# Expert layer: three of the four pieces of the down product as three float32r products each

## The reference, cut to what matters

```
def _moe(x, gate_w, w1, w2, w3):
    ...
    rw, sel = jax.lax.top_k(logits, TOP_K)
    rw = jax.nn.softmax(rw.astype(jnp.float32), axis=-1).astype(x.dtype)
    ...
    for e in range(E):
        we = jnp.sum(jnp.where(sel == e, rw, 0.0), axis=-1)
        h = jax.nn.silu(xf @ w1[e].T) * (xf @ w3[e].T)
        out = out + h @ w2[e].T * we[:, None]
```

## Time and profile before

| | |
|---|---|
| median of 3 runs | 3040.33 us (3038.86 to 3045.66) |
| the profiled execution: its own time | 3042.93 us |
| the profiled execution: span from first to last instruction | 3041.2 us |
| TensorE, share of the span busy | 94% |
| VectorE, ScalarE, GpSimd | 75%, 61%, 23% |
| start of `experts` in the span | 2311.7 us |

### The profile page before, as it was taken

The page is one execution under the profiler, slowest core; times in us unless marked ns, Lnnn a source line. Parts: engine busy times, 40 slices in busy tenths (PEclk is TensorE's granted clock), DMA queues, the critical chain, the costliest instruction groups (busy, mean ns, idle before and its releaser), DMA issues. The chain is left out here.

```text
span 3041.2 us, 62526 instructions
## 1 busy us (share of the span) xinstructions
PE 2866.5 (94%) x22877; PEld 1805.0 (59%) x22878; DVE 2282.8 (75%) x4028; ACT 1867.4 (61%) x3491; POOL 689.7 (23%) x964
## 2 busy tenths in 40 slices
PE   5999999986999999999999999998978999999997
PEld 4777777774333333333333333336767888888886
DVE  5777776774999999999999999976876555555553
ACT  3666666662888888888888888885533222222221
POOL 2222222222000000000000000001102555555554
PEclk7899998986999999999999999998889999999999
DMA  1223322224222222222222222216742333333332
GB/s 46 84 98 112 110 99 98 103 79 131 60 74 72 87 67 67 66 73 72 67 63 71 72 70 67 64 44 189 238 137 73 51 52 50 50 52 50 50 52 37
DMA packets 170749, 243.11 MB, mean 80 GB/s; under 512 B 30920, under 2 KB 118240, under 8 KB 170512
## 3 DMA queue, kind: packets, MB, share of 16 engines
q1 hardware_dynamic: 121920, 170.57, 18.0%
q0 software_dynamic: 31152, 52.33, 8.7%
q10 hardware_dynamic: 17440, 16.98, 1.7%
HBM read 126.53 MB, written 111.21 MB: 78 GB/s over the span
## 5 line engine op out<-in xcount | busy, mean ns | idle before, releaser
L1030 DVE TENSOR_REDUCE b_mxq<-b_p_m 128x1 f32<-128x1024 f32 x1024 | 1220.8, 1221 | 76.3 <-PE b_p_m L1057 67.1
L964 ACT ACTIVATE b_probs<-b_p_e 128x512 f32<-128x512 f32 x2048 | 1105.8, 597 | 140.4 <-PE b_p_e L1110 36.6
L1057 PE MATMUL b_p_m<-b_kst,b_qst 64*128 64x512 f32 x1536 | 568.2, 449 | 0.8 <-DVE b_mxq L1030 0.8
L1110 PE MATMUL b_p_e<-b_qst,b_kst 64*128 64x512 f32 x1536 | 559.9, 444 | 0.2 <-ACT b_probs L964 0.2
L1082 PE MATMUL b_p_o<-b_probs,b_vst 128*32 128x256 f32 x6160 | 481.9, 390 | 0.5 <-ACT b_probs L964 0.4
L1110 PEld LDWEIGHTS b_p_e<-b_qst,b_kst 64*128 64x128 f32 x1536 | 236.4, 184 | 312.5 <-ACT b_probs L964 266.1
L1851 ACT COPY d_hT<-d_p_h 128x512 f32<-128x512 f32 x136 | 79.8, 587 | 401.4 <-PE d_p_h L1944 386.6
L1082 PEld LDWEIGHTS b_p_o<-b_probs,b_vst 128*32 128x32 f32 x6160 | 126.3, 108 | 243.6 <-issue 133.1
L1821 POOL DMA_INDIRECT out_dram<-d_y,d_to x136 | 217.7, 1601 | 199.5 <-DVE d_y L1895 97.4
L1952 PE MATMUL d_p_y<-w2T,d_hT 128*128 x1088 | 257.1, 379 | 1.5 <-ACT d_hT L1851 1.5
L1057 PEld LDWEIGHTS b_p_m<-b_kst,b_qst 64*128 64x128 f32 x1536 | 234.0, 185 | 15.8 <-DVE b_mxq L1030 12.4
(11 more groups left out here) (317 smaller groups left out, 4582.4 us busy)
## 6 DMA issues: line engine op xcount, KB each, us to landing
b_qst<-qk_d SPq DMA_DIRECT2D x288, 64.0 KB
b_kst<-qk_d SPq DMA_DIRECT2D x288, 64.0 KB
qk_d<-a_hi SPq DMA_DIRECT2D x32, 512.0 KB, 2.8
qk_d<-a_lo SPq DMA_DIRECT2D x32, 512.0 KB, 3.8
v_d<-a_v_s SPq DMA_DIRECT2D x16, 1024.0 KB, 4.6
o_d<-b_oT POOLq DMA_DIRECT2D x63, 256.0 KB, 2.7
b_vst<-v_d SPq DMA_DIRECT2D x48, 256.0 KB
raw<-in_L_ffn_w_dram SPq DMA_DIRECT2D x24, 512.0 KB, 5.1
```

The costliest lines, as they stand in the source:

```text
L964: nc.scalar.activation(probs[(2 * step + e % 4 // 2) % BUFS][:, (e % 2) * 512:(e % 2 + 1) * 512], p_e[(slot(e) if more1 else e) % EB][:], ...
L1030: V_.reduce_max(mxq[half][:, h, qt:qt + 1], p_m[j % 2][:], AX.X).then_inc(s["m_red"], 1)
L1057: mm(p_m[j % 2][:, kh * 512:(kh + 1) * 512], qst[r][rows(h), qt * P:(qt + 1) * P], kst[r][rows(h), kh * 512:(kh + 1) * 512], start=True, s ...
L1110: mm(p_e[u % EB][:], kst[r][rows(h), kt * P:(kt + 1) * P], qst[r][rows(h), a * 512:(a + 1) * 512], start=True, stop=True).then_inc(s["e_ps ...
```

## The change

1. `SPLIT = 3`. For the pieces k = 0, 1, 2 the down product is made of three float32r products: rounded hT by rounded w2, rounded hT by the rest of w2, rest of hT by rounded w2. The piece k = 3 stays one float32 product.
2. The rounded parts and rests of w2 (`w2_hi`, `w2_lo`) are made at the beginning of `experts`: ScalarE rounds 768 columns of each expert into a scratch (`rounded`) and copies them back into `w2_hi`, VectorE subtracts. `w2_hi` is declared in the place that `w2T` was declared in, so the fourth piece is still read as `w2T`.
3. ScalarE's copy of the transposed `h` becomes two: 128 columns plain, 384 columns rounded. VectorE gets a new step for each tile, `transposed_low`, that subtracts the rounded part from what is in PSUM. `down` waits for it (`hT_lo`).
4. `act_s`, `h` and `hT` have one buffer instead of two. The small tiles lie in the `raw` buffers of earlier stages. So the Silu waits for the product before it (`h_done`), and `product(m)` for `inner_transposes(m-1)` (`hT_ps`).
5. VectorE's order for a tile is evacuate(m-2), product(m), transposed_low(m-1), scaled(m+2), shared(m+2).

```
+    SPLIT = 3
+    w2_hi = sb("w2_hi", [P, NE, I // P, D], f32r)
+    w2_lo = sb("w2_lo", [P, NE, SPLIT, D], f32r)
-    act_s, h = [sb(f"act{r}", [P, I]) for r in range(2)], [sb(f"h{r}", [P, I]) for r in range(2)]
-    hT = [sb(f"hT{r}", [P, 4, P]) for r in range(2)]
+    hT = sb("hT", [P, 2, SPLIT, P], f32r)
+    hT_hi, hT_lo = hT[:, 0], hT[:, 1]
+    act_s, h = raw[1][:, 0:I], raw[1][:, I:2 * I]
+    rounded = [raw[1][:, 0:SPLIT * D].bitcast(f32r), hT[:].rearrange("p a k t -> p (a k t)")]
...
     def _(act):
+        def weights(e):
+            if e > 1:
+                act.wait_ge(s["w2_rest"], e - 1)
+            nc.scalar.copy(rounded[e % 2], w2T[:, e, 0:SPLIT].rearrange("p k n -> p (k n)")).then_inc(s["w2_round"], 1)
+        def weights_back(e):
+            act.wait_ge(s["w2_rest"], e + 1)
+            nc.scalar.copy(w2_hi[:, e, 0:SPLIT].rearrange("p k n -> p (k n)"), rounded[e % 2].bitcast(f32)).then_inc(s["w2_done"], 1)
+        for e in range(NE):
+            if e > 1:
+                weights_back(e - 2)
+                act.wait_ge(s["w2_done"], e - 1)
+            weights(e)
+        weights_back(NE - 2)
+        weights_back(NE - 1)
+        act.wait_ge(s["w2_done"], NE)
...
         def activated(m, r):
             act.wait_ge(s["up_ps"], 2 * m + 1)
-            nc.scalar.activation(act_s[r][:], p_up[r][:, 0], ACT.Silu).then_inc(s["act_done"], 1)
+            act.wait_ge(s["h_done"], m)
+            nc.scalar.activation(act_s, p_up[r][:, 0], ACT.Silu).then_inc(s["act_done"], 1)
         def transposed(m, r):
             act.wait_ge(s["hT_ps"], m + 1)
-            nc.scalar.copy(hT[r][:], p_h[:]).then_inc(s["hT_done"], 1)
+            nc.scalar.copy(hT_whole, p_h[:, SPLIT:4])
+            nc.scalar.copy(hT_hi, p_h[:, 0:SPLIT]).then_inc(s["hT_done"], 1)
...
     def _(dve):
+        for e in range(NE):
+            dve.wait_ge(s["w2_round"], e + 1)
+            V_.tensor_tensor(w2_lo[:, e].rearrange("p k n -> p (k n)"), w2T[:, e, 0:SPLIT].rearrange("p k n -> p (k n)"), rounded[e % 2].bitcast(f32), ALU.subtract).then_inc(s["w2_rest"], 1)
...
         def product(m, r):
             dve.wait_ge(s["act_done"], m + 1)
             dve.wait_ge(s["up_ps"], 2 * m + 2)
-            V_.tensor_tensor(h[r][:], act_s[r][:], p_up[r][:, 1], ALU.mult).then_inc(s["h_done"], 1)
+            dve.wait_ge(s["hT_ps"], m)
+            V_.tensor_tensor(h, act_s, p_up[r][:, 1], ALU.mult).then_inc(s["h_done"], 1)
+        def transposed_low(m):
+            dve.wait_ge(s["hT_done"], m + 1)
+            V_.tensor_tensor(hT_lo, p_h[:, 0:SPLIT], hT_hi.bitcast(f32), ALU.subtract).then_inc(s["hT_lo"], 1)
...
-                product(m, q % 2)
                 if not first or q > 1:
                     evacuate(m - 2, (q + 2) % 4)
+                product(m, q % 2)
+                if not first or q > 0:
+                    transposed_low(m - 1)
...
         def down(m, r, e):
             pe.wait_ge(s["hT_done"], m + 1)
+            pe.wait_ge(s["hT_lo"], m + 1)
             pe.wait_ge(s["y_done"], m)
-            for k in range(4):
-                last = mm(p_y[:, 0:D], hT[r][:, k], w2T[:, bass.ds(e, 1), k, :].rearrange("p o n -> p (o n)"), start=(k == 0), stop=(k == 3))
+            for k in range(SPLIT):
+                for j, (a, w) in enumerate(((hT_hi, w2_hi), (hT_hi, w2_lo[:]), (hT_lo, w2_hi))):
+                    mm(p_y[:, 0:D], a[:, k], w[:, bass.ds(e, 1), k, :].rearrange("p o n -> p (o n)"), start=(k == 0 and j == 0), stop=False)
+            for k in range(SPLIT, 4):
+                last = mm(p_y[:, 0:D], hT_whole[:, k - SPLIT], w2T[:, bass.ds(e, 1), k, :].rearrange("p o n -> p (o n)"), start=False, stop=(k == 3))
             last.then_inc(s["y_ps"], 1)
```

More of the change, by code:

```diff
@@ L1760, in _, with experts @@
                 column(e * per + i)
-def experts(nc, ctx, ident, xg_d, up_hi, up_lo, w2T, ln2_w, token_of, pick, expert_of, out_d, TILES):
+def experts(nc, ctx, ident, xg_d, up_hi, up_lo, w2T, raw, ln2_w, token_of, pick, expert_of, out_d, TILES):
     P, D, I, NE = 128, 256, 512, 8
@@ L1774, in sb @@
         return ctx.enter_context(nc.sbuf_tensor("d_" + name, shape, dt))
[L1776 to L1779, removed]
+    SPLIT = 3
+    w2_hi = sb("w2_hi", [P, NE, I // P, D], f32r)
+    w2_lo = sb("w2_lo", [P, NE, SPLIT, D], f32r)
     xh, xl = [sb(f"xh{r}", [P, 2, P], f32r) for r in range(2)], [sb(f"xl{r}", [P, 2, P], f32r) for r in range(2)]
-    act_s, h = [sb(f"act{r}", [P, I]) for r in range(2)], [sb(f"h{r}", [P, I]) for r in range(2)]
-    hT = [sb(f"hT{r}", [P, 4, P]) for r in range(2)]
-    y = [sb(f"y{r}", [P, D]) for r in range(2)]
+    hT = sb("hT", [P, 2, SPLIT, P], f32r)
+    hT_hi, hT_lo = hT[:, 0], hT[:, 1]
+    act_s, h = raw[1][:, 0:I], raw[1][:, I:2 * I]
+    y = [raw[2][:, r * D:(r + 1) * D] for r in range(2)]
+    hT_whole = raw[2][:, 2 * D:2 * D + (4 - SPLIT) * P].rearrange("p (k t) -> p k t", k=4 - SPLIT)
+    xs = [raw[2][:, 640:640 + D + 2], *(raw[0][:, r * (D + 2):(r + 1) * (D + 2)] for r in range(3))]
+    small = raw[0][:, 3 * (D + 2):]
+    ln2, ids = small[:, 0:2], small[:, 2:8].bitcast(i32)
+    tok, to = [ids[:, r:r + 1] for r in range(4)], [ids[:, 4 + r:5 + r] for r in range(2)]
+    part, share = [small[:, 8 + 2 * r:10 + 2 * r] for r in range(4)], [small[:, 16 + r:17 + r] for r in range(4)]
+    rounded = [raw[1][:, 0:SPLIT * D].bitcast(f32r), hT[:].rearrange("p a k t -> p (a k t)")]
     p_x = ctx.enter_context(nc.psum_tensor("d_p_x", [P, 4, P], f32))
@@ L1913, in _ @@
         round(TILES // 4 - 1, False, 2)
-        for m in (TILES - 2, TILES - 1):
-            evacuate(m, m % 4)
+        evacuate(TILES - 2, 2)
+        transposed_low(TILES - 1)
+        evacuate(TILES - 1, 3)
     @block.tensor
@@ L1943, in inner_transposes @@
             for k in range(4):
-                last = tr(p_h[:, k, :], h[r][:, k * P:(k + 1) * P], ident[:])
+                last = tr(p_h[:, k, :], h[:, k * P:(k + 1) * P], ident[:])
             last.then_inc(s["hT_ps"], 1)
@@ L1966, in round @@
                 up(m, r, e)
+                if first and q == 2:
+                    pe.wait_ge(s["w2_done"], NE)
                 if not first or q > 1:
@@ L2012, in layer_kernel @@
                                 ln1_w, wq, wk, wv, x1_d, norm, qk_d, v_d, pair0, B)
-        raw = [sb(f"raw{j}", [P, 1024]) for j in range(3)]
+        raw = [sb(f"raw{j}", [P, 1024])[:] for j in range(3)]
         slots = sb("slots", [P, 2 * NT])
@@ L2025, in layer_kernel @@
             up_hi, up_lo = (weights.enter_context(nc.sbuf_tensor(n, [P, NE, 2, D // P, I], mybir.dt.float32r)) for n in ("up_hi", "up_lo"))
-            w2T = weights.enter_context(nc.sbuf_tensor("w2T", [P, NE, I // P, D], f32))
+            down = ExitStack()
+            w2T = down.enter_context(nc.sbuf_tensor("w2T", [P, NE, I // P, D], f32))
             with Stage(nc) as stage:
                 invert_places_and_transpose_weights(nc, stage, ident, ones_r, lower_r, slots, counts, raw, token_of, pick, expert_of, w1, w3, w2, up_hi, up_lo, w2T, NT, TILES)
+            down.close()
             with Stage(nc) as stage:
-                experts(nc, stage, ident, xg_d, up_hi, up_lo, w2T, ln2_w, token_of, pick, expert_of, out_d, TILES)
+                experts(nc, stage, ident, xg_d, up_hi, up_lo, w2T, raw, ln2_w, token_of, pick, expert_of, out_d, TILES)
 _INS = ["L0_attn_x", "L0_attn_Wq", "L0_attn_Wk", "L0_attn_Wv", "L0_attn_Wg", "L0_attn_Wgk1", "L0_attn_Wgk2",
```

28 lines of the change are left out of this document (14 added, 14 removed).

## The result

The changed kernel took 3023.43 us in the median of 4 runs (3017.12 to 3027.36), the kernel before 3041.56 (3038.86 to 3045.66). The ratio is 0.9937, with a 95% interval from 0.9915 to 0.9959: faster by 0.63%, where 0.7% and 3020 us had been forecast. The profiled execution took 3027.36 us, its span is 3025.6.

The account below looks back on a forecast made before the run. TensorE was taken to bound the last stage, 5.19 us per tile. From the profiled 3042.93 us, minus 29.1 (down products) plus 8.0 (beginning) gave 3021.8; the median, 2.6 lower, 3019.2, stated as 3020, range 3011 to 3033.

Parts of the forecast that it names:

- The down product: TensorE, each tile of the last stage: 1.50 us in place of 1.72, saving 29.1 us over 134 tiles.
- the rival of short products that the sequencer can't issue fast enough: TensorE's down product: nine more instructions cost 1.2 us per tile, making the kernel slower at 3210 us; chance 0.06.
- The shorter price: Down product by the skill's 109 ns per 256-column product: another 0.09 us saved per tile, sum some 12 us lower.
- The waits and the new VectorE step: Single-buffer waits and transposed_low in each tile: cost nothing, covered by up, with 1.55 us least slack; subtraction 0.55 us.
- The beginning: Start of `experts`: ScalarE's sixteen copies and VectorE's subtractions delay scaled(0) and the whole stage by 8.0 us.
- The table load: ScalarE, beginning of `experts`: 1.28 us, ending with the last copies back at about 2326.4, ahead of the first Silu.
- The pauses at lap tops: TensorE's sequencer late from three expert-number loads: 1.36 us in each of 16 laps, 22 us, kernel at 3042; chance 0.08.
- my case: Whole kernel: tile of 4.97 us with TensorE busy 100 of 100, beginning 8.0 us later, 3020 us; chance 0.78.
- A load's price: TensorE's register loads at lap tops: by the skill's 600 ns, three take 1.8 us, showing 0.2 per lap, 3 in all.
- The ring of scatters: GpSimd's scatters become the bound if landings beside gathers exceed 4.10 us: 3048 at 4.32, 3073 at 4.5; chance 0.05.
- My argument that slow landings would show in the period: Against scatters becoming the bound: landings beside gathers today can't exceed 4.3 us, or the tile period would show it.

Follow-up runs that it names:

- Waits only: The kernel before with only single `act_s`, `h` and `hT`, their two new waits and VectorE's new order: 3042.57 us, ratio 1.0005.
- loads late: The changed kernel with two of TensorE's three expert-number loads at a lap's top moved behind the first up product: 3011.75 us, 0.9900 of the kernel before.
- early inputs: The changed kernel with VectorE splitting the first two inputs behind the third and fifth subtraction of weights: 3021.06 us, 0.9934 of the kernel before.
- both: The changed kernel with later expert-number loads at lap tops and earlier splits of the first two inputs: 3008.56 us, 0.9899 of the kernel before.

## Why the prediction was right

- **The down product**, forecast at 1.50 us from the 256-column products of the first stage (0.119 each): measured 1.51. The whole forecast hangs on this term, 29 us, and it held. So the rival of short products that the sequencer can't issue fast enough is out: they start 0.12 us apart, though their addresses come from registers.
- **The shorter price** of 109 ns for 256 columns, which the Trainium skill gives ("TensorE: Matmul & The Clock Gate", Back-to-back issue gap), would have made it 1.41 us by an estimate of 0.43 + 9 x 0.109. The trace shows 119, and the measurement decides.
- **The waits and the new VectorE step** at nothing: right. Forecast 1.55 us of slack, measured 1.53; the subtraction 0.55, measured 0.56. Waits only shows the buffers' part by itself, in the kernel before.
- **The beginning**, forecast 8.0 us: measured 7.9. ScalarE's copies take 0.83 us and 1.60 from one expert to the next (1.61 forecast). The table load was misplaced: I took it to end at 2326.4, but it stands behind the wait for up(0) and runs only then. It delayed the first product of VectorE by a quarter us against the kernel before and TensorE not at all.
- **The pauses at lap tops** were a rival with a chance of 0.08 and a price of 22 us. They came, with 9.9 us. This is the step that failed: I held my case and this rival to exclude each other, and my case has TensorE busy 100 of 100 us, where 98.5 were measured. Its mechanism, a fixed number and not a time, is what the traces show. Its price was wrong in the reserve: I counted a dozen products, 1.61 us, and the queue held 17 records, 2.19 us. Against it stood 2.97 us for three loads, and the sequencer needed 2.93. That agreement is luck: a load costs 0.65 and not 0.99, and the rest is the jump and register work, which I had left out.
- **A load's price.** That a load takes 0.65 us agrees with the Trainium skill ("DMA: Bandwidth & Descriptors", Latency and other measured facts), which has about 600 ns at least. By it I had 3 us over the stage, from loads of 1.8 us against a reserve of 1.61; both sides of that comparison were too small.
- **Up** got 0.055 us shorter per tile, some 7.4 us over the stage, not forecast by any case. It hid most of the pauses: -29.1 - 7.4 + 9.9 + 7.9 + 0.3 (the end) = -18.4, and the stage shows -18.2. The forecast for the stage was -29.1 + 8.0 = -21. That it came so near is in part luck: two things that it left out, +9.9 and -7.4, nearly cancel.
- **The ring of scatters** didn't become the bound, but its margin is smaller than the 0.3 us that I took. At the end, where no gathers are left, scatters stand 4.65 us apart in the chain. Beside gathers, and when they are behind, they stand 4.8 apart, here in loads late, against a tile of 4.91:

```profile
2909.39 1.60 POOL L1828 DMA_INDIRECT out_dram<-raw  x1 [1.02 <-DMA out_dram<-raw]
2914.22 1.60 POOL L1828 DMA_INDIRECT out_dram<-raw  x1 [1.02 <-issue]
2919.02 1.60 POOL L1828 DMA_INDIRECT out_dram<-raw  x1 [1.01 <-issue]
```

  So a ring that has fallen behind wins back 0.1 us per tile. In the changed kernel's trace one landing near the end took 5.14 us, the next scatter came 6.05 us behind the last, and the ring didn't catch up before the end: hence eight scatters in the chain in place of three, for 0.3 us. Loads late, early inputs and both have three. My argument that slow landings would show in the period was wrong as well: in the kernel before, the scatter that follows the last one of the earlier trace rows starts at 2608.78, 6.49 us behind it, and every tile stays at 5.18 or 5.19.

## What to carry to other kernels

A float32 product that is split into three float32r products costs 3 x 0.119 us against 0.43 at 256 columns, here: take such a price from a stage of the same trace that already issues products of the same columns and type, and then ask what the shorter products no longer hide. An engine's sequencer that loads numbers from SBUF lives on the work queued ahead of it, and here that was a number of records and not a time: shorter products make the same queue last less long. Put only the load that the next product needs at a loop's top, and the others behind a long product. Compare the stage and not the program, when the stages ahead of it vary by more than the change is worth.

## What the runs showed of the hardware

- A load of a number from SBUF by TensorE's sequencer with its register instructions costs 0.65 us, and is hidden only as far as products are queued.
- When the sequencer came to the end of a lap, 17 records of products were handed over and not yet started, in every kernel of this study, whatever they were; a float32 product counts as two. They lasted 3.12 us with 8 down records among them, 2.49 with 10, 2.19 with 11. A jump back and three loads took the sequencer 2.93 us in the last case.
- The same float32r products of 512 columns started 0.241 us apart on average in one kernel and 0.236 in the other. Moving the stationary tile by 32 bytes changed it by 0.002 to 0.003, down onto a multiple of 64 bytes and up off one; the rest isn't explained.
- After 2.05 us of idle time at the beginning of the stage the granted clock fell to half in one execution, and stood at half for at least 6 us; in another kernel, where TensorE reached full clock later and idled less, it didn't. In the changed kernel with two loads more TensorE paused for about 2 us at 14 lap tops, and the clock fell behind one of them alone.
